# A decoder kernel on Trainium2: row gathers of the first mixture sent in groups of four behind PE's up products

## Time and profile before

| | |
|---|---|
| median of three runs | 1641.85 us (1641.39 to 1643.27) |
| the profiled execution | 1646.56 us, span 1644.7 us |
| PE busy | 1302.2 us, 79% of the span |
| DVE busy | 1169.2 us, 71% |
| POOL busy | 823.7 us, 50% |
| ACT busy | 725.7 us, 44% |
| chain by engine | PE 41%, DVE 23%, issue 14%, POOL 12%, ACT 6%, another core or an unknown queue 1% |
| mean granted PE clock | 0.911 of 2.4 GHz |

### The profile page before, as it was taken

The page is one execution under the profiler, slowest core; times in us unless marked ns, Lnnn a source line. Parts: engine busy times, 40 slices in busy tenths (PEclk is TensorE's granted clock), DMA queues, the critical chain, the costliest instruction groups (busy, mean ns, idle before and its releaser), DMA issues.

```text
span 1644.7 us, 41193 instructions
## 1 busy us (share of the span) xinstructions
PE 1302.2 (79%) x15406; PEld 889.4 (54%) x15406; DVE 1169.2 (71%) x2520; ACT 725.7 (44%) x1486; POOL 823.7 (50%) x1030
## 2 busy tenths in 40 slices
PE   7979878877788868689998887592988873798881
PEld 4656545656555656456665455491555543455550
DVE  6977859874688847578887485333778852798875
ACT  3544435544455534234444354160455521355555
POOL 4543357752566725435453453506466624456654
PEclk9999989997999969789999999796999987899995
DMA  9000000000000000000000000112100012000000
GB/s 336 0 1 1 0 1 0 0 2 21 0 1 0 0 2 13 0 6 1 0 0 1 1 0 26 37 33 84 52 0 1 0 38 36 4 0 2 0 1 26
DMA packets 19559, 29.95 MB, mean 18 GB/s; under 512 B 4291, under 2 KB 16323, under 8 KB 18714
## 3 DMA queue, kind: packets, MB, share of 16 engines
q1 hardware_dynamic: 17562, 24.97, 4.4%
q0 software_dynamic: 1920, 3.94, 1.4%
HBM read 23.91 MB, written 4.98 MB: 18 GB/s over the span
## 4 chain that ended last, share of the span: by engine, by line
PE 41%; DVE 23%; issue 14%; POOL 12%; ACT 6%; another core or an unknown queue 1%; DMA 1%; POOLq 0%; DVEq 0%; ACTq 0%; SPq 0%
PE ps L333 32%; DVE maxima L430 6%; PE ps L453 4%; DVE arena L432 4%; PE ps L825 3%; ACT arena L440 2%; DVE heads_out L765 2%; POOL arena L910 2%; POOL arena L525 2%; POOL inv_norm L905 2%; DVE sq_sum L1039 1%; POOL arena L1938 1%; DVE gate L1795 1%; POOL arena L2226 1%
## 5 line engine op out<-in xcount | busy, mean ns | idle before, releaser
L333 PE MATMUL ps<-arena 64*64 64x64 f32 (+5 forms) x7921 | 387.6, 281 | 36.5 <-issue 12.1
L333 PEld LDWEIGHTS ps<-arena 64*64 64x64 f32 (+4 forms) x7921 | 241.3, 135 | 167.4 <-issue 130.9
L525 POOL TENSOR_TENSOR arena<-arena,w_const 128x1024 f32<-128x1024 f32 x96 | 182.3, 1901 | 150.4 <-DVE arena L755 67.0
L430 DVE TENSOR_REDUCE maxima<-ps 128x16 f32<-128x1024 f32 (+1 forms) x144 | 158.5, 1101 | 56.2 <-PE ps L333 52.2
L440 ACT ACTIVATE arena<-arena 128x1024 f32<-128x1024 f32 (+1 forms) x144 | 138.5, 962 | 128.1 <-DVE arena L432 127.4
L453 PE MATMUL ps<-w_const,arena 128*128 128x128 f32 x1024 | 144.2, 283 | 51.3 <-ACT arena L440 34.4
L905 POOL TENSOR_TENSOR inv_norm<-sq_floor,minus_half 128x16 f32<-128x16 f32 x32 | 121.9, 3810 | 86.4 <-DVE sq_floor L1042 86.3
L432 DVE TENSOR_TENSOR arena<-ps,maxima 128x1024 f32<-128x1024 f32 (+1 forms) x144 | 159.3, 1106 | 4.9
L453 PEld LDWEIGHTS ps<-w_const,arena 128*128 128x128 f32 x1024 | 116.9, 145 | 73.7 <-ACT arena L440 44.7
L447 ACT COPY arena<-ps 128x1024 f32<-128x1024 f32 (+1 forms) x144 | 131.4, 912 | 54.9 <-PE ps L453 54.5
L371 POOL TENSOR_TENSOR rstd<-var_eps,minus_half 128x1 f32<-128x1 f32 x144 | 80.4, 570 | 145.0 <-DVE var_eps L873 101.3
(11 more groups left out here) (317 smaller groups left out, 2667.6 us busy)
## 6 DMA issues: line engine op xcount, KB each, us to landing
experts<-in_pack_moe SPq DMA_DIRECT2D x2, 4180.0 KB, 20.0
w_fa<-in_pack_fa SPq DMA_DIRECT2D x2, 1024.0 KB, 12.0
moe_in<-state SPq DMA_DIRECT2D x2, 1024.0 KB, 5.3
w_a<-in_pack_a SPq DMA_DIRECT2D x1, 1824.0 KB, 17.1
moe_out<-arena SPq DMA_DIRECT2D x5, 256.0 KB, 2.3
w_fg<-in_pack_fg SPq DMA_DIRECT2D x2, 537.0 KB, 12.5
ctxT<-in_ctxT SPq DMA_DIRECT2D x1, 1024.0 KB, 8.1
out<-state SPq DMA_DIRECT2D x4, 256.0 KB, 2.3
```

The source lines that it names most:

```text
L333: return nc.tensor.matmul(o, lhsT, rhs, start=start, stop=stop, skip_group_check=True)
L430: nc.vector.reduce_max(mx, sc, X_AXIS).then_inc(signal["max_ready"], 1)
L525: nc.gpsimd.tensor_tensor(keys_wide(s).rearrange("p (b h t) -> p b h t", b=SEQS, h=8), key8(s).rearrange("p (b t) -> p b t", b=SEQS).unsqu ...
```

## The change

POOL gets one wait before each of the gathers 8, 12, 16 and 20. The wait is for `m_up` to reach i - 7, that is 1, 5, 9 and 13: PE must have done the up products of tile 0, 4, 8 and 12. Gathers 0 to 7 are sent as before. Nothing else is changed, in this stage or in another.

```diff
@@ -1928,6 +1928,8 @@
             pool.wait_ge(ms["m_x_stored"], 16)
             pool.wait_ge(ms["m_chosen"], TOKENS)
             for i in range(SORTED):
+                if i >= 8 and i % 4 == 0:
+                    pool.wait_ge(ms["m_up"], i - 7)
                 nc.gpsimd.indirect_dma_start(m_sorted[:, i * P:(i + 1) * P], None, moe_in,
```

## The result

The changed kernel took 1628.61 us, the median of nine runs (1620.42 to 1631.56), against 1640.17 us for the kernel before in nine runs (1635.02 to 1643.27). The ratio is 0.9927, with a 95% interval of 0.9907 to 0.9947: 12.0 us less (the two medians are 11.6 us apart). A second comparison (experiment 1) gave 0.9895 (0.9866 to 0.9924), 17.2 us less.

A forecast was written before the change was run, and what follows sets the result against it. A long gather series was taken to hold PE's marks in the first mixture. Terms: 13.5 - 1.5 - 3.9 = 8.1 us less, from the median 1641.85 to 1633.8 us (chance 0.40); range 1624 to 1645.

The forecast's parts named there:

- What bounds the loop: First mixture: PE's marks reach ACT and DVE late while POOL's 23 gathers go on; a 17.06 us piece in the chain.
- Rival D: First mixture's stall isn't the gathers' doing, is shorter unprofiled, or its gain goes to the low clock: some 1641 us; chance 0.18.
- The first wait: POOL's wait before gather 8 for tile 0's up products: moves that gather by 0.3 us, the first twelve staying one series.
- The release: ACT's ReLU of tile 2 goes on 4.56 us after gather 11 starts, at 1056.8 against 1070.34: 13.5 us earlier.
- a piece of an unknown queue of 3 to 4 us: Sign that the forecast is right: such a piece in the changed kernel's chain of waits, where 17.06 us stood before.
- The next late step: After the release, the fourth weight copy and tile 3's up products no longer hide in the stall: 1.5 us of loss.
- the clock: PE's clock level after the shorter stand: taken as nothing, with 2.4 us gain to 4.2 us loss kept for the range.
- The three series: The later series of 4, 4 and 3 gathers beside PE work cost 1.3 us each, 3.9 us in all.
- Rival B: Every series holds PE's marks to its end, spreading the stall over the steady part: 1649.4 us; chance 0.12.
- The rows in time: Gathers 12 to 15 need 8.0 us and have 9.4 us before their turn, so they are covered by 1.4 us.
- Rival C: Rows come late because each gather waits a whole DVE copy: 1.4 us a series, 4.1 us in all, 1637.9 us; chance 0.08.
- rival A: Short series cost nothing and PE's clock holds: gain 16.7 us, time 1625.2 us; chance 0.22.

The follow-up runs named there:

- experiment 1: The changed kernel run again without an edit, five rounds beside the kernel before: ratio 0.9895 to the kernel before.
- experiment 2: Changed kernel with its four waits asking for the landing of the four gathers sent just before, not for PE's up products: ratio 0.9900 to the kernel before.
- experiment 3: Changed kernel with only one wait, before gather 12, so series of twelve and eleven gathers: ratio 0.9960 to the kernel before.
- experiment 4: Changed kernel with only the wait before gather 8 left, for the first up product: ratio 0.9982 to the kernel before.
- experiment 10: The 23 gathers replaced by plain transfers that SP sends in pairs, sorting left out, on experiment 9's chip: ratio 0.9880 to the kernel before.
- experiment 9: The kernel before, unedited, profiled again on a third chip: ratio 1.0006, at 1639.7 us for the kernel before in that comparison.
- experiment 6: Changed kernel with a wait before every second gather from the eighth on (pairs), where the kernel before took 1621.1 us: ratio 0.9988 to it.
- experiment 7: Changed kernel with a wait before each gather from the eighth on (singles), where the kernel before took 1621.1 us: ratio 0.9999 to it.
- experiment 12: The singles kernel again, a wait before each gather from the eighth on, where the kernel before took 1620.8 us: ratio 1.0003 to it.
- experiment 5: Kernel before with one wait more: PE's first turn waits until the last of the 23 gathers has landed; ratio 1.0160 to the kernel before (1621.1 us).
- experiment 8: The 23 gathers replaced by plain transfers that SP sends in pairs, sorting left out, where the kernel before took 1621.1 us: ratio 1.0001 to it.

## Why the prediction was right, and where its sizes were off

**What bounds the loop.** The inference that PE's marks are held by a long series of gathers is shown by experiments 2, 3 and 4: pauses that don't wait for PE bring the gain, a second long series brings back a hold of its own, and a break of 0.79 us brings no gain. Experiment 10 adds that plain transfers in pairs do no harm. The number of gathers in a row isn't all of it, though: twelve in a row at the start held the mark of tile 2 by about 1 us (see the release below), while eleven beside the full loop (experiment 3) made ACT wait 3.94 and 4.67 us. What else counts, the density of PE's work or that of the gathers, no run tells. Rival D is refuted for the chips that hold. On a chip without a hold the changed kernel itself wasn't run; its variants with pairs and singles stayed within 0.2% there, as D says.

**The first wait** did what the text said, nearly: it moved gather 8 by 0.5 us, not 0.3, and alone it is worth 0.2% (experiment 4), an amount that can't be told from nothing.

**The release** was mis-sized. I carried over 4.56 us from the start of the last gather to the release. It was 2.19 us in the changed kernel (1045.28 to 1047.47), 2.5 in experiment 1, 3.0 and 3.1 behind the two series of experiment 3, and 4.4 in experiment 9. So the ReLU of tile 2 came 15.7 us earlier against the first turn (25.7 to 10.0), not 13.5. That is almost the bound of 15.8 for "nothing held at all". On chips without a hold this ReLU comes 9.0 to 9.1 us after the first turn (experiments 6, 7 and 12), so about 1 us of hold was left, and the sign that the text named, a piece of an unknown queue of 3 to 4 us, isn't in the chain. The last packets of the series start between 1047 and 1048, beside the ReLU's start, so this trace can't tell a mark that the series' end released from one that was hardly held. One reading was off too: in the kernel before ACT and DVE go on 0.3 to 0.5 us after the end of the slice from 1069 to 1070, but the last packet in it ends at 1069.20, so it was 1.1 to 1.3 us after the packets.

**The next late step and the clock** were put at a loss of 1.5 and at nothing. With the loop's gain of 16.7 us, the 15.7 of the release and the loss at the series below, they came to 16.7 - 15.7 + 1.2 = 2.2 us of gain together. The clock was at 1.00 from 1047.5 on, so the term that I had kept for the range only (2.4 us) belonged in the sum: the shorter stand did not bring the low level back. That leaves some 0.2 us for the late step, and not 1.5.

**The three series** were put at 1.3 us each. They cost 0.48, 0.47 and 0.23 us in the first profile (8.06, 8.05 and 7.81 against 7.58), 1.2 in all and not 3.9. In experiment 1 they cost 2.4 us (8.58, 8.59 and 8.01). A mark is late by about a microsecond there, but the loop absorbs part of it. DVE's weight copies in the changed kernel show it: the second of these lines starts 2.88 us after the first, where the steady pace is 1.79.

```profile
1053.97 0.70 DVE L2156 COPY arena<-experts 128x1028 f32 x1 [0.93 <-PE ps L333]
1056.85 0.70 DVE L2156 COPY arena<-experts 128x1028 f32 x1 [2.18 <-PE ps L333]
1057.78 0.70 DVE L2156 COPY arena<-experts 128x1028 f32 x1 [0.23 <-PE ps L333]
```

Rival B, a hold to the end of each short series, didn't happen: the eleven in a row of experiment 3 brought it, four did not.

**The rows in time.** The last gather of the second series starts at 1055.09, and its turn at 1060.40 follows PE's work without a gap. Rival C fell. In the short series a gather beside DVE's copies took 1.22 us at most, 0.28 more than alone. The rule of the Trainium skill's page "SBUF — State Buffer" (section "Who interferes with whom"), that one waits out the other's whole instruction, would have added up to 0.70; here only part of it was seen. The same section of the Trainium skill says that transfers never contend with a compute engine and that PE never waits on anyone. It speaks of the ports of the on-chip memory, and not of semaphores. Here ACT waited 17.08 and 17.82 us for PE's mark beside gathers in the two profiles of the kernel before, and 10.01 us in experiment 4, so for the marks the measurement decides.

**The time.** The terms give 8.1 us; the measured gain is 12.0 us in the first comparison and 17.2 in the second. The loop's own gain, 16.7 and 15.1 us, fits the second. What makes the first smaller isn't settled: no profile of one of its slower runs is at hand. The forecast and rival A (16.7 us, no cost at the series, the clock kept) enclose both but for half a microsecond, and A was nearer in the second. The traces are nearer to A too: the loop's gain in the first profile is A's 16.7 us, although the short series weren't free as A had them. That the forecast's 8.1 us is not far from the first comparison's 12.0 is partly luck: all three of its terms were sized against the change, the release, the late step with the clock, and the series.

## What to carry to other kernels

When one engine goes on late though the record of the engine that it waits for ended long ago, look for what else was in flight over the same stretch, and for when that ended: the profile named an unknown queue, and the cause stood in POOL's timeline. In this stage the gathers that POOL sends beside dense PE work did best in groups of two to four with pauses of 1.3 to 4.7 us; a wait for PE's progress and one for the gathers' own landing did equally well, and the rows still came in time. And a gain of this kind must be measured on more than one chip, since kernels with such pauses gained 12 to 22 us on some and nothing clear of noise on others.

## What the runs showed of the hardware that was not expected

The hold depends on the chip. On the chips of experiments 5 to 8 and of experiment 12 the kernel before took 1621 us (29 and 17 runs), and in every other comparison 1639.7 to 1642.5. The two kinds don't overlap: the slowest of the ones took 1627.5 us, the fastest of the others 1633.8. Each chip was measured on one occasion only, so that it is the chip and not the occasion is inferred. The traces of the two kinds differ in two more things. The first is in the second mixture, whose gathers no edit touches. There ACT's second step starts 1.71 us after its up product began in the kernel before and 1.77 us in experiment 9. This delay is 1.7 to 1.8 us in five of the nine profiles where the kernel before took some 1640 us, and 1.05 or 1.06 us in all five where it took 1621. So a series of five held a mark by some 0.7 us too, in some executions.

The second is the records of landing marks, from which the profile works out a gather's time to landing. It has that time on a chip without a hold (experiment 12, median 2.6 us), and not in experiment 9, on a chip with one:

```profile
arena<-moe_in,arena POOLq DMA_INDIRECT x28, 2.6
```

```profile
arena<-moe_in,arena POOLq DMA_INDIRECT x28
```

In the kernel before 10 to 42 of the 64 landing marks of each of the first four groups were recorded, while the rows did arrive; experiments 5 and 6 have all 64. SP's stores beside the gathers lack records too: of the first store's 16 marks the changed kernel's trace has 3, experiment 6 all. But the chip alone doesn't do it: in experiment 10, on the chip of experiment 9 and with no gather in the first mixture, all marks of the plain transfers are there, and the second mixture's five gathers have their time to landing (3.2 us). So on the chips with a hold something is amiss with other marks beside the gathers too, or with their records, and not with PE's alone. Whether the two have one cause, and what it is, none of these runs tells.
